# First pair: the loads of the next two x blocks ahead of the loads for the next diagonal matrices in SyncE's queue

## What is computed

```python
x = x + einsum('bct,bcd->bdt', x, L0_weights[adapter])          # 64x64 mix of the rows of a sample
x = x + (x @ W1 + (x @ A1[adapter]^T) @ B1[adapter])            # rank 16
x = x + (x @ W2^T + 0.5 * (x @ A2[labeler]^T) @ B2^T)           # rank 32
x = x + (x @ W3^T + 2.0 * sum_e gate_e * (x @ A3[e]^T) @ B3[e]) # 8 experts, top 2 of the logits x @ Wr^T
```

## Time and profile before

| what | us |
|---|---|
| median of 3 runs | 548.06 (547.38 to 548.61) |
| the profiled execution's own time | 548.72 |
| its span | 546.9 |
| PE busy in the span | 535.2 (98%) |
| DVE / ACT / POOL busy | 252.1 / 162.6 / 156.9 |
| mean granted TensorE clock | 0.997 of full speed |

### The profile page before, as it was taken

The page is one execution under the profiler, slowest core; times in us unless marked ns, Lnnn a source line. Parts: engine busy times, 40 slices in busy tenths (PEclk is TensorE's granted clock), DMA queues, the critical chain, the costliest instruction groups (busy, mean ns, idle before and its releaser), DMA issues.

```text
span 546.9 us, 9086 instructions
## 1 busy us (share of the span) xinstructions
PE 535.2 (98%) x2812; PEld 476.6 (87%) x2812; DVE 252.1 (46%) x609; ACT 162.6 (30%) x314; POOL 156.9 (29%) x247
## 2 busy tenths in 40 slices
PE   7999999999999999999979999999999999999996
PEld 6999999999999999999868788888888888888885
DVE  3841322132311111214957675674756647567463
ACT  4641312121111111115623433333323333233322
POOL 2501000000001000354651744435444344443400
PEclk9999999999999999999998999999999999999999
DMA  8803020034251111120230331323313233132312
GB/s 283 292 25 130 2 77 16 1 134 149 73 178 48 40 38 44 38 82 1 61 127 2 111 117 40 108 80 110 115 38 109 78 113 112 40 107 78 112 33 77
DMA packets 24060, 46.76 MB, mean 85 GB/s; under 512 B 7636, under 2 KB 13396, under 8 KB 23908
## 3 DMA queue, kind: packets, MB, share of 16 engines
q1 hardware_dynamic: 23844, 45.85, 25.1%
q0 software_dynamic: 192, 0.59, 0.3%
HBM read 33.39 MB, written 13.04 MB: 85 GB/s over the span
## 4 chain that ended last, share of the span: by engine, by line
PE 91%; SPq 2%; DMA 2%; DVE 1%; POOL 1%; issue 1%; ACT 1%; POOLq 0%; DVEq 0%; ACTq 0%
PE bank L1276 26%; PE bank L1310 25%; PE bank L1227 15%; PE bank L1296 7%; PE bank L1366 4%; PE bank L1358 4%; PE bank L1243 4%; PE bank L1374 1%; PE bank L1361 1%; PE bank L1360 1%; DMA w2raw<-in_w_dram 1%; SPq L413 1%; PE bank L1320 1%; DMA raw<-in_x_dram 1%; SPq L430 1%
## 5 line engine op out<-in xcount | busy, mean ns | idle before, releaser
L1276 PE MATMUL bank<-e_lo,w1t_hi 128*128 128x488 f32 (+2 forms) x240 | 86.9, 362 | 0.0
L1276 PE MATMUL bank<-e_hi,w1t_hi 128*128 128x488 f32 (+2 forms) x240 | 86.8, 362 | 0.0
L1276 PE MATMUL bank<-e_hi,w1t_lo 128*128 128x488 f32 (+2 forms) x240 | 86.7, 361 | 0.0
L897 DVE TENSOR_TENSOR w1t_lo<-raw,w1t_hi 128x1024 fp32r<-128x1024 f32 x18 | 25.6, 1421 | 81.1 <-ACT w1t_hi L656 60.0
L1227 PE MATMUL bank<-g_hi,w2s_hi 128*128 128x384 f32 (+1 forms) x144 | 48.3, 336 | 0.3 <-DVE e_lo L897 0.3
L1276 PEld LDWEIGHTS bank<-e_lo,w1t_hi 128*128 128x128 f32 x240 | 45.2, 188 | 3.9
L1276 PEld LDWEIGHTS bank<-e_hi,w1t_hi 128*128 128x128 f32 x240 | 45.0, 188 | 4.0
L1276 PEld LDWEIGHTS bank<-e_hi,w1t_lo 128*128 128x128 f32 x240 | 45.1, 188 | 3.9
L1227 PE MATMUL bank<-g_lo,w2s_hi 128*128 128x384 f32 (+1 forms) x144 | 48.2, 335 | 0.0
L1227 PE MATMUL bank<-g_hi,w2s_lo 128*128 128x384 f32 (+1 forms) x144 | 48.2, 335 | 0.0
L897 DVE TENSOR_TENSOR e_lo<-bank,e_hi 128x384 fp32r<-128x384 f32 (+1 forms) x24 | 13.0, 558 | 60.7 <-ACT e_hi L691 60.7
(11 more groups left out here) (233 smaller groups left out, 1332.3 us busy)
## 6 DMA issues: line engine op xcount, KB each, us to landing
raw<-in_x_dram SPq DMA_DIRECT2D x16, 512.0 KB, 3.4
out_dram<-ost SPq DMA_DIRECT2D x32, 256.0 KB, 2.1
b1s<-b1scr SPq DMA_DIRECT2D x32, 217.5 KB, 2.8
raw<-in_b1w_dram SPq DMA_DIRECT2D x10, 512.0 KB, 3.2
w2raw<-in_w_dram SPq DMA_DIRECT2D x7, 512.0 KB, 7.9
graw<-in_w3a3wr_dram SPq DMA_DIRECT2D x4, 768.0 KB, 8.7
graw<-in_w3a3wr_dram SPq DMA_DIRECT2D x8, 196.0 KB, 7.3
b1scr<-b1stage_hi SPq DMA_DIRECT2D x8, 192.0 KB
```

The lines of the kernel that those rows point to most:

```text
L897: V.tensor_tensor(dst, src, f32(hi), ALU.subtract).then_inc(signal, 1)
L1276: ins = nc.tensor.matmul(stage_bank(u, j)[:, 0:WIDTH[c]], W1T[u][a][:, k, :], EX[c][z][:, k, :], start=(k == 0 and (a, z) == TERMS[0]), st ...
```

## The change

In `pair_io` of pair 0 the wait for `s_pl` and the two loads of x stand ahead of the four loads into `bdraw`, which stood ahead of them before. The other pairs keep their order. Nothing is added or taken away.

```diff
+            def load_x(p):
+                for s in range(2):
+                    sp.dma_start(raw[s][:, :, :], x[bass.ds(2 * p + 2 + s, 1)].rearrange("a p k t -> p (a k) t")).then_inc(s_raw[s], 16)
+
             def pair_io(p, last):
+                first = isinstance(p, int) and p == 0
+                if first:
+                    sp.wait_ge(s_pl, 3)
+                    load_x(0)
                 if not last:
                     for s in range(2):
                         sp.wait_ge(s_idx, 48)
                         sp.wait_ge(s_bd, 2 * p + s + 1)
                         load_w0(2 * p + 2 + s, s)
-                    if isinstance(p, int) and p == 0:
-                        sp.wait_ge(s_pl, 3)
-                    else:
+                    if not first:
                         sp.wait_ge(s_sum, 4 * p)
                         sp.wait_ge(s_opl, OPS * p + (5 - OPS))
-                    for s in range(2):
-                        sp.dma_start(raw[s][:, :, :], x[bass.ds(2 * p + 2 + s, 1)].rearrange("a p k t -> p (a k) t")).then_inc(s_raw[s], 16)
+                        load_x(p)
```

## The result

| | before | after |
|---|---|---|
| median, first set of runs | 547.72 us (4 runs, with one more than the forecast had; 546.96 to 548.61) | 543.95 us (4 runs, 543.65 to 544.38) |
| span of the profiled execution | 546.9 | 542.6 |
| its own time | 548.72 | 544.38 |

The ratio of the times is 0.992, with a 95% interval of 0.9903 to 0.9938: 4.4 us faster, 3.4 to 5.3. The two medians lie 3.8 apart, inside that interval. The forecast gain was 5.2. The changed kernel ran three more times, in two further sets, with ratios of 0.9916 (0.9899 to 0.9933), 0.9923 (0.9901 to 0.9944) and 0.9907 (0.9876 to 0.9937). The forecast was 542.9 in a range of 542.1 to 544.6. The time lies in the range, on its upper side, where the rival "DVE is held by POOL" stood at 544.0.

A forecast was written before the change was run, and what follows sets the result against it. PE bounds the kernel, busy 98% of the span, so only its standstill and slow stretch could pay: 3.7 + 1.6 - 0.1 = 5.2 us off 548.06 gives 542.9 us, range 542.1 to 544.6.

The forecast's parts named there:

- DVE is held by POOL: Rival at `h1_across` and `h2_across`: POOL's SBUF instructions block DVE's, PE waits 0.5 us, 1.2 in all; 544.0 us, chance 0.17.
- What binds: PE's single wait between 262 and 300 us, 3.5 us at `mixed(1, 1)`, comes from SP issuing `bdraw` loads before x.
- First term: At `mixed(1, 1)`: with x issued 5.0 us earlier, PE's standstill goes altogether, 3.7 us.
- Second term: From `mixed(1, 1)` to `h1_into(1, 1)`: the half-speed clock behind the standstill goes too, 1.6 us.
- Landing at 3.53: Loads of x into `raw`: issued at 275.7, x takes the same 3.53 us and lands at 279.2.
- What is late next: DVE's chain to `h1c` and `h2c` fits by 0.2 and 0.3 us; nothing to 0.2 us set against the gain.
- x late: Rival at the `raw` loads: x, issued right behind `b1s`, lands later than 279.2; 543 to 545.5 us, chance 0.05.
- clock: Rival behind `mixed(1, 1)`: the clock falls all the same, only the 3.7 us come back; 544.4 us, chance 0.05.
- no change: Rival: the transfer queue holds x back the whole 5 us, or PE waits as long for something hidden; 548.1 us, chance 0.04.
- slower: Rival at POOL's `diagonal(2)`: the `bdraw` loads land far too late behind x; 549 us and up, chance 0.03.

## Why the prediction was right, and where it was off

- **What binds** was right: the only PE wait between 262 and 300 us was owed to SP's queue, through ACT's and DVE's order. Moving one load by 4.9 us took it away, moving it by less took away less, and block 2 alone was enough.
- **First term, 3.7 us.** Came in full: `mixed(1, 1)` 0.23 behind its predecessor.
- **Second term, 1.6 us.** Came in full: the granted clock is 1.00 through the stretch. The ground I gave for it, that the fall goes with the long standstill, is borne out by the counts above (45 of 49 executions before, none of 19 after), though not every long standstill brings it. The 1.6 us are the loss of one execution: 4 of 49 lost nothing and 18 about twice as much, so as a term of the median it was taken from a case that happened to be the middle one.
- **Landing at 3.53.** Mis-sized: 3.6 to 4.5 in four profiles. I called the way clear because the transfer engines moved nothing from 277.0 to 277.5. But x is now issued at 275.8, and the trace of before shows what is under way from then on, the loads of `b1s` (two of 217.5 KB; the DMA share is the number before the last):

```profile
275.50:276.00 0.50, 0.50 (x4) 0.42 (x3) 0.44 (x3) 0.00 (x0) 0.50 (x2) 1.00 0.87 168
276.00:276.50 0.50, 0.50 (x4) 0.42 (x3) 0.43 (x3) 0.00 (x0) 0.35 (x1) 1.00 0.79 232
276.50:277.00 0.50, 0.50 (x4) 0.38 (x4) 0.47 (x2) 0.00 (x0) 0.00 (x0) 1.00 0.42 133
```

  With two or three loads ahead, x is issued at 277.9 or later and was ready after 3.4 to 3.6 us. That the `b1s` loads make the difference is likely, and no run tests it; one of the four landings behind them took 3.6 as well. The landing stayed inside the margin of 1.4 for PE. But it seems to act at a place where I had not looked: who is first between DVE and POOL.
- **"What is late next" was mis-sized.** I took 3.0 us for DVE from `xn_lo` to `h1c` as safe and 2.29 for `t3`, and set 0.1 against the gain. From the start of `xn_lo` to the end of `h1c` it measured 282.46 to 286.16, 3.7, in the long case and 3.1 in the short one; `t3` 3.13 and 2.57. The loss was 1.1 us or about 0.1. The 3.0 was no undisturbed time either: in the earlier trace rows it holds a `gw` of 0.55, which takes 0.16 elsewhere. With POOL's subtractions held back the same instructions took 2.6 us (282.73 to 285.36).
- **The rival "DVE is held by POOL"** had place, mechanism and price: 0.5 us at `h1_across` and 1.2 in all forecast, 0.3 and 1.1 measured. It got a chance of 0.17. In two of four profiles it is what happened. My reason against it was that the `gate` sum would have to wait for one subtraction only. It overlooked the two `gm` products ahead of `gate`, the second of which meets the first subtraction, so that `gate` meets the second one. The Trainium skill, page "SBUF — State Buffer", section "Who interferes with whom", lists `tensor_scalar`, the operation of the `gm` products, among those that can take the shared path when their operands allow it; the trace agrees: 1.06 for the pair beside POOL, 0.48 without.
- **The median.** The forecast was 542.9 for one case. The kernel is a mixture of two, with spans of 541.3 and 542.4 to 542.6, against 541.7 forecast for the one. The medians of its four groups of runs are 543.95, 543.34, 544.0 and 543.6; how many executions fall in which case is open, since the setup alone moves a time by as much. That the time lies in the range is owed to its width, which took in the rival at 544.0: the first median is within 0.1 us of the rival's figure and 1.05 above mine. The mechanism of the gain was right; the loss set against it, 0.1 us, was too small for half of the profiles.
- **The rivals "x late", "clock", "no change", "slower"** did not happen. POOL asked for `bdraw` at 298.97; its last load was issued at 281.3 and the four took at most 3.2 us to land. Only the wait of PE failed to come for "x late"; the landing itself was late, as said.

## What to carry to other kernels

Where a queue issues several transfers, the order of issue should follow who waits first, not which wait was satisfied first; the one load that somebody waits for is worth all the others' issue time, and a standstill of TensorE can cost its length and a slow stretch behind it (3.5 and 1.6 us here). When such a standstill goes, add up the margins of what comes next with the neighbours it will newly run beside: margins of 0.2 to 0.3 us were less than one instruction of the other engine. And before two profiles of two kernels are compared, look whether one kernel's own executions fall into cases, by a second profile and by the clocks of the executions that have none.

## What the runs showed that I had not expected

- DVE and POOL trade whole instructions, and 0.2 us or less seem to decide: the same two instructions took 3.13 and 1.28 us, or 2.57 and 3.34, in executions of one kernel.
- A later landing went with a shorter time: x ready after 4.3 to 4.5 us with spans of 541.3, after 3.6 to 4.1 with 542.4 to 542.6, in four profiles of the changed kernel.
- The granted clock stayed full over standstills of 0.9 and 2.1 us, even with 1.1 more close behind, and fell to 0.50 behind one of 2.7, after work had begun again. In 4 of 49 executions of the kernel before it did not fall at all.
